# Fused attention, output product and convolution on one core: which projection tiles of a head pair are made one unit ahead, and in which pairs

## The reference

```python
scale, shift = split(cond @ W_emb + b_emb)
xn  = rms_norm(x) * g_norm * (1 + scale) + shift
q, k, v = split_heads(xn @ W_qkv)             # 16 heads of 64
q, k = rms_norm(q) * g_q, rms_norm(k) * g_k
o   = softmax(q @ k.T / 8) @ v
x   = x + o + o @ W_out
out = x + causal depthwise conv(x, 4 taps = cond) + b
```

## Time and profile before

| | |
|---|---|
| median of 3 runs | 2486.0 us (2485.43 to 2486.32) |
| the profiled execution | 2484.39 us |
| its span, first to last instruction | 2482.6 us |
| span taken by units 0 to 7 | from 137.7 to 666.7 us, some 64 to 69 us each |
| PE / DVE / ACT / POOL busy | 95% / 84% / 74% / 26% |
| PE's mean granted clock | 0.988 of full speed |

### The profile page before, as it was taken

One profiled execution on the slowest core, in us unless ns is written; L12 is line 12 of the kernel. 1 busy time (PEld: TensorE's weight loads), 2 busy tenths in 40 slices (PEclk: granted clock), 3 DMA queues, 4 the chain that ended last, 5 costly groups with the idle time before them and its releaser, 6 DMA issues.

```text
span 2482.6 us, 54243 instructions
## 1 busy us (share of the span) xinstructions
PE 2365.0 (95%) x20794; PEld 1526.7 (61%) x20794; DVE 2090.6 (84%) x3368; ACT 1829.1 (74%) x2834; POOL 640.5 (26%) x451
## 2 busy tenths in 40 slices
PE   4799999999899999999999999999999999999899
PEld 0455555555466666666666666666666666666688
DVE  7768988888778888888888988888888888888876
ACT  5467778888777777878777787777777777777632
POOL 1122323332233222332232223233222222222100
PEclk9899999999999999999999999999999999999999
DMA  9999999999998989999999999989988888888971
GB/s 365 296 216 227 194 182 193 181 188 227 197 203 180 197 182 212 181 199 225 197 217 182 204 195 194 184 189 228 201 174 169 182 171 170 167 161 164 181 188 52
DMA packets 1234737, 484.99 MB, mean 195 GB/s; under 512 B 1139632, under 2 KB 1197872, under 8 KB 1232048
## 3 DMA queue, kind: packets, MB, share of 16 engines
q1 hardware_dynamic: 1234480, 481.53, 92.1%
HBM read 137.20 MB, written 56.66 MB: 78 GB/s over the span
## 4 chain that ended last, share of the span: by engine, by line
PE 63%; DVE 20%; issue 5%; ACT 4%; SPq 3%; DMA 2%; ACTq 0%
PE proj L1014 32%; PE scores L956 10%; DVE neg L1542 9%; PE values L975 9%; PE proj L1039 8%; DVE p_pair L1551 7%; ACT p_pair L1193 2%; SPq L762 2%; DVE bias L1545 2%; PE proj L1044 1%; PE misc L1056 1%; ACT late L1185 1%; DMA w_sb<-w_dram 1%; SPq L718 1%; PE values L990 1%
## 5 line engine op out<-in xcount | busy, mean ns | idle before, releaser
L1014 PE MATMUL proj<-w_sb,xn_sb 128*128 128x384 f16 x6144 | 1035.2, 327 | 24.4 <-DMA w_sb<-w_dram 14.1
L1185 ACT ACTIVATE late<-scores,bias,l_scale 128x1024 f32<-128x1024 f32 x512 | 617.3, 1206 | 347.9 <-DVE bias L1545 329.4
L1014 PEld LDWEIGHTS proj<-w_sb,xn_sb 128*128 128x128 f16 x6144 | 587.5, 98 | 428.5 <-issue 28.8
L1551 DVE TENSOR_TENSOR p_pair<-late,p_pair 128x1024 f16<-128x1024 f32 x512 | 616.8, 1246 | 125.9 <-ACT p_pair L1193 125.8
L1542 DVE TENSOR_REDUCE neg<-scores 128x1 f32<-128x1024 f32 x512 | 623.2, 1217 | 109.4 <-PE scores L956 106.3
L1193 ACT ACTIVATE p_pair<-late 128x1024 f16<-128x1024 f32 x512 | 511.7, 1052 | 0.0
L975 PE MATMUL values<-pT,v_pair 128*64 128x256 f16 x6144 | 390.9, 278 | 14.7 <-ACT inv_row L1253 14.7
L956 PE MATMUL scores<-late 64*128 64x512 f16 x3072 | 377.6, 379 | 15.4 <-ACT late L1185 13.1
L975 PEld LDWEIGHTS values<-pT,v_pair 128*64 128x64 f16 x6144 | 319.5, 111 | 94.8 <-issue 70.9
L1458 POOL TENSOR_TENSOR rs<-ms,power 128x16 f32<-128x16 f32 x63 | 183.0, 2905 | 403.6 <-DVE ms L1565 403.3
L1039 PE MATMUL proj<-late,wo 128*128 128x256 f16 x2304 | 267.7, 273 | 1.5 <-issue 1.5
(11 more groups left out here) (181 smaller groups left out, 2026.8 us busy)
## 6 DMA issues: line engine op xcount, KB each, us to landing
w_sb<-w_dram SPq DMA_DIRECT2D x121, 384.0 KB, 4.1
o_dram<-oT_pair SPq DMA_DIRECT2D x124, 128.0 KB, 2.4
out<-late SPq DMA_DIRECT2D x54, 256.0 KB, 2.9
x_in<-in_x SPq DMA_DIRECT2D x25, 512.0 KB, 4.5
late<-in_x SPq DMA_DIRECT2D x25, 512.0 KB, 4.2
wq_raw<-in_L_cond_W_qkv SPq DMA_DIRECT2D x8, 1536.0 KB, 10.7
late<-o_dram SPq DMA_DIRECT2D x12, 1024.0 KB, 6.0
xn_dram<-late SPq DMA_DIRECT2D x21, 512.0 KB, 3.6
```

The costliest lines, as they stand in the source:

```text
L1014: last = nc.tensor.matmul(proj[:, t % 2, 0:6 * DH], xn_sb[:, t, i * K + c, :], w_sb[:, c, j, :], start=(c == 0 and i == j == 0), stop=(c = ...
L1185: nc.scalar.activation(prob[:, h, :], scores[:, h, :], ACT.Exp, bias=bias[:, s:s + 1], scale=const["l_scale"][:, 0:1], accum_out=total[:, ...
L1551: nc.vector.tensor_tensor(p_pair[:, s % 4, 1, :], prob[:, h, :], p_pair[:, s % 4, 0, :], ALU.subtract).then_inc(lo_done, 1)
```

## The change

In units 0 to 6 three tiles of w + 1 are made instead of two, and they are spread: tile 0 in pair 5, tile 1 in pair 6, tile 2 in pair 7 (one half before `score(u, 7)`, one half after). Units 1 to 7 project only the tiles 3 to 7 of w, in pairs 0 to 4. From tile 2 on, the two banks are swapped for w = 2 to 8, so tile 1 and tile 2 use the same bank. `load_w` moves from pair 5 to pair 4 in SP's program. ACT's readings move with the tiles: tile 7 of w from the start of pair 5 to the end of pair 4 (units 1 to 7), tiles 0 and 1 of w + 1 to the end of pairs 5 and 6, tile 2 to the start of the next pair 0.

```diff
         later_quarters = (
-            ((2, 0, 4), (3, 0, 1)),
-            ((3, 1, 4), (4, 0, 2)),
-            ((4, 2, 4), (5, 0, 3)),
-            ((5, 3, 4), (6, 0, 4)),
-            ((7, 0, 4),),
+            ((3, 0, 4), (4, 0, 1)),
+            ((4, 1, 4), (5, 0, 2)),
+            ((5, 2, 4), (6, 0, 2)),
+            ((6, 2, 4), (7, 0, 2)),
+            ((7, 2, 4),),
             (), (), (),
         )
+
+        early_quarters = (
+            (), (), (), (), (),
+            ((0, 0, 4),),
+            ((1, 0, 4),),
+            (),
+        )
+
+        def bank_of(w, t):
+            return (t + 1) % 2 if 2 <= w <= K and t >= 2 else t % 2
...
-                    if p == 5:
-                        if more:
-                            for i in range(4 if gives_early(u) else 2):
-                                load_w(w + 1, i)
+                    if p == (4 if gives_early(u) else 5) and more:
+                        for i in range(4 if gives_early(u) else 2):
+                            load_w(w + 1, i)
...
             def project(w, t, q0, q1, fins=None):
                 if q0 == 0:
-                    need(pe, qkv_ev, K * w + t - 1)
                     early = has_early(w - 1)
+                    need(pe, qkv_ev, K * w + t - (0 if early and t in (0, 2) else 1))
                     if early and t == 1:
                         pe.wait_ge(h_ev, 3 * w - 1)
-                    elif t == (2 if early else 0):
+                    elif t == (3 if early else 0):
                         need(pe, h_ev, 3 * w)
...
                     if gives_early(u) and p == 7:
-                        project(w + 1, 0, 0, 4)
+                        project(w + 1, 2, 0, 2)
...
                     if qkv and p == 7:
                         if gives_early(u):
-                            project(w + 1, 1, 0, 4)
+                            project(w + 1, 2, 2, 4)
...
+                    if gives_early(u):
+                        for t, q0, q1 in early_quarters[p]:
+                            project(w + 1, t, q0, q1)
...
                     if p == 0:
                         if has_early(u):
-                            read_projection(w, 1)
+                            read_projection(w, 2)
...
                     if p == 5:
                         if qkv:
-                            read_projection(w, 7)
+                            if not has_early(u):
+                                read_projection(w, 7)
                             squares(w, 1, (h_ss, 2 * w + 1))
...
-                    if gives_early(u) and p == 7:
-                        read_projection(w + 1, 0)
...
                     if p == 0 and qkv:
-                        read_projection(w, 2 if has_early(u) else 0)
+                        read_projection(w, 3 if has_early(u) else 0)
                     if p == 1 and has_early(u):
-                        read_projection(w, 3)
+                        read_projection(w, 4)
+                    if p in (5, 6) and gives_early(u):
+                        read_projection(w + 1, p - 5)
...
-                            read_projection(w, 4 if has_early(u) else 3)
+                            read_projection(w, 5 if has_early(u) else 3)
...
-                        read_projection(w, 5)
+                        read_projection(w, 6 if has_early(u) else 5)
...
-                            read_projection(w, 6)
+                            read_projection(w, 7 if has_early(u) else 6)
```

More of the change, by code:

```diff
@@ L1013, in project @@
                     for i, j in ((0, 0), (0, 1), (1, 0)):
-                        last = nc.tensor.matmul(proj[:, t % 2, 0:6 * DH], xn_sb[:, t, i * K + c, :], w_sb[:, c, j, :],
+                        last = nc.tensor.matmul(proj[:, bank_of(w, t), 0:6 * DH], xn_sb[:, t, i * K + c, :], w_sb[:, c, j, :],
                                                 start=(c == 0 and i == j == 0), stop=(c == K - 1 and i == 1))
@@ L1201, in read_projection @@
                 nc.scalar.activation(stage[:, hf, 2 * (t % KH):2 * (t % KH) + 2, :],
-                                     proj[:, t % 2, 0:6 * DH].rearrange("p (h n) -> p h n", h=2), ACT.Copy,
+                                     proj[:, bank_of(w, t), 0:6 * DH].rearrange("p (h n) -> p h n", h=2), ACT.Copy,
                                      scale=QKV_DOWN).then_inc(qkv_ev, 1)
```

## The result

The changed kernel takes 2541.3 us (median of 5 runs, 2536.0 to 2543.7) against 2486.2 us before: a ratio of 1.022, with a 95% interval of 1.0208 to 1.0232. The profiled execution took 2541.32 us; its span is 2539.5, 56.9 more than before. The prediction was 2526, in a range of 2508 to 2544.

What follows compares the result with a forecast made beforehand. A ring of DVE and ACT, not PE, was taken to set the pace. Terms 21.6 - 1 + 7.5 + 8.4 + 3 = 39.5 on 2484.4, plus 1.6 to the median, gave 2526 us, range 2508 to 2544.

Steps and rivals of the forecast that it cites:

- The ring: DVE and ACT alternate on maxima, exponentials, high and low parts, 7.71 us a pair; PE must only have scores ready.
- Pair 7: Units 0 to 6: half tile and scores wait for ACT's reading of tile 1, 3.8 us before cover; together 21.6.
- The small waits at pair 0: DVE's small waits at the next pair 0 go, as only half a tile follows the scores: -1.
- Pair 5: Tile 0 waits for ACT's reading of tile 7 and for weights, so scores of pair 6 come late: 7.5, 2 to 13.
- Unit 7: Tiles that come by DMA are wanted a pair earlier while `load_xn` isn't moved: +8.4, between 4 and 11.
- The clock: After idle stands PE may run slower at tile 0 in pair 5 and the half tile in pair 7: 3, bounds 0 and 24.
- PE's idle time was the price: Faster rival: readings come early enough and the change fills PE's gaps, 2476 us; 5%.
- Milder: Rival: only pair 7 costs; weights land by the median and unit 7 only trades its wait, 2510 us; 17%.
- Worse: the clock falls at both places: Rival: in nearly every unit, and the loads take their longest, 20 us more, 2546; 15%.
- the waits for `stage`: Sign: PE's wait for ACT's copy appears on `proj` in pairs 5 and 7, 2 to 3 us each.
- Waits for rows: Sign: in unit 7 waits for `xn_sb` stand in pairs 0 to 2, 8 us or more in all.
- the two signs of being wrong: DVE doesn't wait in pair 7, or the waits for weights in pair 5 come to over 3 us a unit.

Runs made afterwards that it cites:

- e1: Changed kernel with tile 2 wholly behind the scores of pair 7 instead of half ahead of them: 2509.2 us.
- e7: Changed kernel without the swap of banks: tile 2 goes to tile 0's bank, the queries' transposes of pair 7 to tile 1's: 2512.4 us.
- e10: Kernel before with only the weight loads moved from pair 5 to pair 4 in units 0 to 6: 2481.4 us, ratio 0.9978.
- e2: Changed kernel with 11 extra unread matmuls of 512 columns in PE's wait ahead of the half tile of pair 7: 2526.9 us.
- e6: Changed kernel with unread matmuls in PE's stands of pair 5, ahead of tile 0 (9) and of the scores (12, not in unit 0): 2534.8 us.
- e4: Changed kernel with the rows for tiles 4 to 6 of the next batch loaded sooner, in units 6 (pairs 5, 7) and 7 (pair 0): 2526.3 us.
- e5: Changed kernel with the four weight loads of each early unit back in pair 5 of SP's program: 2604.7 us.
- e3: Changed kernel with ACT reading tile 1 ahead of `high_halves` and `o_high` in pair 6 instead of behind them: 2522.3 us.

## Why the prediction was right, and where a size was off

- *The ring sets the pace, and PE's idle time in units 0 to 7 costs nothing unless it stands ahead of scores.* Right: e1 and e7 confirm it with the distances forecast (7.7 and 9.0 us), and e10 with the time.
- *Pair 7, 21.6 us.* Right in mechanism and size: 32.3 measured, of which 9.9 are the clock's (e2), so 22.4. "In unit 3 this place is where the copy of the inverses starts now" was exact: the half tile started 8.12 us after the maximum of pair 6 (420.96 - 412.84), and 395.7 - 387.62 = 8.08 was forecast.
- *The small waits at pair 0, -1.* Measured -1.7.
- *Pair 5, 7.5 us (2 to 13).* 19.2 measured, 10.2 with the stands filled (e6). For units 4 and 5 nothing was forecast; it cost 1.4 and 0 us in this execution, 0.1 and 1.5 in that of e4, so the 0 in unit 5 is luck.
- *Unit 7, +8.4 (4 to 11).* 10.4 measured; e4 shows that the loads were all of it. The clock is in it as well, which the prediction did not count here: after the 7.42 us of waiting 12 matmuls took 4.00 us instead of 2.12. An estimate from the lengths of the tiles and scores behind the two waits for rows, against those in the kernel before, is some 3 us of the 10.4.
- *The clock, 3 us (0 to 24).* This is the step that failed in size. "I take 3, since the stand before the half tile is only the rest of pair 6, shorter than the one in the earlier trace rows": the stand was shorter, 2.51 against 3.45 us, and the clock fell all the same in six units of seven. It came to 9.9 in pair 7 and up to 9.0 in pair 5, some 19, inside the bounds but six times the term. The trace of the kernel before spoke against the reason, in a row that the prediction doesn't show: in unit 6, after a stand of 2.75 us, a tile took 5.74 us, as long as the one in the earlier trace rows.

```profile
584.61 5.74 PE L1014 MATMUL proj<-w_sb,xn_sb 128*128 128x384 f16 x24 [2.75 <-DMA w_sb<-w_dram]
```

- *The sum.* The terms as measured, 22.4 - 1.7 + 10.2 + 10.4 + 18.9 - 0.7 - 2.5 = 57.0, make the 56.9. With 19 in place of 3 the forecast would have been 2542. That this comes so near is partly luck: pair 5 and unit 7 cost 4.7 us more than forecast besides, and 3.2 us that nobody forecast (-0.7 elsewhere, -2.5 at the end) take most of it back. As it stands, the forecast was 15 us short, and 2541 lies 3 us below the end of the range.
- *Rivals.* "PE's idle time was the price" wanted a faster kernel and fell with the result; e10 shows the same on the kernel before. "Milder" fell with pair 5 and unit 7. "Worse: the clock falls at both places", 15% at 2546, was nearest to what came, nearer than the forecast with its 60%.
- What was to be seen: the waits for `stage` in pair 7 are there; in pair 5 PE waited for the weights instead (2.54 us in unit 3), as ACT's reading came first. DVE's waits were to grow to 45 us and grew to 74.7. DVE's wait at pair 7 was to be some 4 us and was 5.5 in six units; units 2 to 5 were to last some 4 us longer and lasted 7.4, 8.3, 7.0 and 4.0 longer. Waits for rows of 8 us or more came as 12.3. Of the two signs of being wrong, DVE did wait in pair 7, and the waits for weights in pair 5 were 12.5 us in all, over 3 us in unit 0 alone (3.6).

## What to carry to other kernels

Ask of each idle stretch who waits behind it. The engine with the highest busy share can idle for nothing while a ring of two others sets the pace; the waits of *those* engines for the one outside the ring are the most that can be gained, here 13.7 us, and 10 of it were had by issuing loads sooner. Even among those a wait can cost little, as DVE's 11.1 us for `misc` seem to have. Before putting work into an engine's gap, look at what stands behind it in that engine's order and where in the other engine's order its buffer is given back; and price the stands that a plan makes on TensorE twice, once as time and once as the lower clock after them.

## What the runs showed of the hardware

- After a stand of 2.5 us ahead of the half tile TensorE ran it at the lower clock in six units of seven in the changed kernel, and in 22 of 28 over the four executions with this stand (the changed kernel, e4, e5, e6); in unit 3 of the first, 12 matmuls of 384 columns took 3.54 us instead of 2.12. Which units it hits differs between executions of the same code. After a stand of 1.17 us (e3) all seven half tiles kept their time.
- Filling the stand with 77 matmuls whose result nobody reads made the kernel 14 us faster (2541.3 to 2526.9); 9.9 of it are read off the half tiles.
- Moving four weight loads one pair sooner in SyncE's order (e10) took away all 14.1 us of PE's waits for them and 5 us of the time. A wait of PE for transposes appeared beside it (5.5 us in three places), its longest for transposes issued ahead of those loads.
